# Where an expert block's bias enters PSUM: from a TensorE product to a ScalarE copy

## The chip, the cores and the metric

The kernel runs on one core of one Trainium2 chip. Its time is the device time of one execution in microseconds (us), given as the median of several runs. The profile is of one execution of its own, whose time stands beside its span below. PE is TensorE, ACT ScalarE, DVE VectorE, POOL GpSimd and SP SyncE.

## The reference

Two layers work on x (4 x 512 tokens, 512 channels): a gate and a Mamba2 mixer, a gate and a mixture of experts, a gate and grouped causal attention, a gate and a gated feed-forward network. The change touches the mixture of experts alone (8 experts, each token goes to its two best):

```python
logits = x @ gate_w.T + gate_b
top_vals, top_idx = jax.lax.top_k(logits, TOP_K)
routing = jax.nn.softmax(top_vals.astype(jnp.float32), axis=-1).astype(x.dtype)
for e in range(E):
    h = x @ w1[e].T + b1[e]
    x_glu = h[:, 0::2]
    x_lin = h[:, 1::2]
    y = x_glu * jax.nn.sigmoid(1.702 * x_glu) * (x_lin + 1.0)
    ye = y @ w2[e].T + b2[e]
    we = jnp.sum(routing * (top_idx == e), axis=-1)
    out = out + ye * we[:, None]
```

## The kernel before, in words

One core does the whole program; each engine has its own instruction list, written out by hand, and the lists meet at semaphores. The four stages follow one another. Within the expert stage the order is fixed by the Python code: nothing is planned by costs.

**Routing.** The gate logits, the top two and the prefix sums give each of the 4096 (token, expert) pairs a slot. The slots are sorted by expert and cut into 39 blocks (`NBLK`) of 128 slots, each of one expert. DVE writes a small integer table `tab` (one column for each block: its expert, the next expert, and a flag that says whether the next expert's weights must be split now). Engines read it with value loads into registers. During this the tokens are stored to DRAM as `u_tok` (SP, L621), behind the loads of the routing constants and of the bias table `bias_f` (L605 and L607).

**A block.** In block j PE (`block_pe`, L2372) does this in order: four transposes of block j's inner values `m_y` into the bank TP; the two up products of block j+1 (`up_glu`, `up_lin`) into banks UG and UL, three of each in turn; a wait for `by_lo` of block j; four transposes of the gathered tokens of block j+2 (`inputs_T`) into the same TP; the down product of block j into the bank DN. Each of the three products (`product`, L2344) is 12 matmuls of 128x128 weights on 512 columns in a split form (high times high, high times low, low times high) and, ahead of them, one bias product (L2345): a selector `sel_e` (which row is the block's expert) times the table `bias_r`. It opens the accumulation with start=True. So there are 39 x 3 = 117 bias products.

ACT (`block_act`, L1000) copies TP to `by_hi` (L1008), takes the tanh of UG into `m_t` (`up_tanh`, L977), copies TP to `bu_hi` (`u_hi_copy`, L981), and copies DN to `m_o` (L1036), which a DMA of its queue stores (L1043). DVE (`block_dve`, L1836) follows each with `by_lo` (L1842), `glu` into `m_t` (L1809), `inner` into `m_y` (L1815), the selector of block j+2 (L1803) and `bu_lo` (L1819), which PE needs for the next block. Where the flag is set, the next expert's weights are split too, in three pieces: the high parts on ACT (L990), the low parts on DVE (L1797), laced between the copies above. With this data these are blocks 0, 4, 18, 22, 23, 27 and 34.

ACT's list is a loop of six blocks (L1054), passed six times, and three blocks behind it; DVE's too (L1887). PE's loop holds three blocks (L2398). In the list of each ACT block stands an If with the weight pieces and an Else without them, and value loads of the table for the block behind (L997 and L998). At the loop's top the first of these loads stand ahead of the first block's `by_hi`: the blocks 0, 6, 12, 18, 24 and 30, and 36 behind the loop, are called heads here.

**Beside it** the recurrence of the next gate runs: scans on DVE (L449, L462), products and sums on POOL, a few copies and exps on ACT, DMAs of the queues of SP and ACT. POOL also gathers the tokens of each block with indirect DMAs (L752). SP loads the weights of each expert into `m_stage` (L616).

Of the kernel before, what the change touches and what calls it, by code (L numbers as in the profile page):

```python
# [19 lines left out]
P = 128  # L20
BATCH, T, C = 4, 512, 512
KC = C // P
# [25 lines left out]
for _name, _n in (("iota", P), ("before", P), ("rst", NT * E), ("rst2", NT * E), ("full", NT), ("blk", 2 * NT), ("place", 1), ("row", 1)):  # L48
    RC[_name] = _at
    _at += _n  # L50
# [41 lines left out]
def network(nc, xT, fT, condT, cols_d, rows_d, w_in_d, w_out_d, moe_d, gw_d, bias_d, rc_d, att_d, ffn_d, outT):  # L92
# [6 lines left out]
    with ctx:  # L99
# [75 lines left out]
        with ExitStack() as s:  # L175
            m_stage = sb("m_stage", [P, MOE_W], F32, s)
            mw = sb("mw", [P, 2, 2, MOE_W], F32R, s)
            ug = sb("ug", [P, 3, C], F32, s)
            bu_hi = sb("bu_hi", [P, KC, P], F32R, s)
            bu_lo = sb("bu_lo", [P, KC, P], F32R, s)  # L180
            m_t = sb("m_t", [P, I_MOE], F32, s)
            m_y = sb("m_y", [P, I_MOE], F32, s)
            by_hi = sb("by_hi", [P, KC, P], F32R, s)
            by_lo = sb("by_lo", [P, KC, P], F32R, s)
            m_o = sb("m_o", [P, 2, C], F32, s)
            sb("pad_b", [P, 256], F32, s)
            bias_r = sb("bias_r", [P, 2 * I_MOE + C], F32R, s)
            sel_e = sb("sel_e", [P, 3, P], F32R, s)
            row_e = sb("row_e", [P, 1], F32, s)
            exp_of = sb("exp_of", [P, NBLK + 1], F32, s)  # L190
            idx = sb("idx", [P, NBLK], I32, s)
            idx_now = sb("idx_now", [P, 3], I32, s)

            tab = sb("tab", [P, 3, NBLK + 1], I32, s)
        with ExitStack() as s:
# [4 lines left out]
            bias_f = sb("bias_f", [P, 2 * I_MOE + C], F32, s)  # L200
# [5 lines left out]
            etab = sb("etab", [P, 3, NBLK + 1], F32, s)  # L206
# [54 lines left out]
        masks_ready, setup_step, setup_mm, setup_act = sem("masks_ready"), sem("setup_step"), sem("setup_mm"), sem("setup_act")  # L261
# [26 lines left out]
        route_mm, route_vec, lg_exp = sem("route_mm"), sem("route_vec"), sem("lg_exp")  # L288
        LGP_DONE, U_DONE, PREFIX_DONE, IDX_DONE = 1, 2, 3, 4
        LG_SUB, MASK_READY, ONEHOT_READY, IDX_READY, TAB_READY = 1, 2, 3, 4, 5  # L290
        m_staged = [sem(f"m_staged{i}") for i in range(M_PIECES)]
        mw_hi_ready, w_split, sel_ready = sem("mw_hi_ready"), sem("w_split"), sem("sel_ready")
# [35 lines left out]
        AT_PREFIX, AT_POSITION, AT_ROWS = 38, 47, 51  # L328
# [16 lines left out]
        def keep_busy(n):  # L345

            for _ in range(n):
                nc.tensor.matmul(SPARE[:].rearrange("p (a l) -> p a l", a=TB), ident_b[:],
                                 causal_b[:].unsqueeze(1).to_broadcast([P, TB, P]), start=True, stop=True)
# [205 lines left out]
        def _(sp):  # L555
# [48 lines left out]
            sp.wait_ge(masks_ready, N_MASKS + 1)  # L604
            sp.dma_start(rc[:], rc_d).then_inc(loaded, 16)  # L605
            for h in range(2):
                sp.dma_start(bias_f[32 * h:32 * h + E, :], bias_d).then_inc(loaded, 16)  # L607

            def stage(e):

                for p in range(M_PIECES):
                    if not isinstance(e, int):
                        sp.wait_ge(w_split, M_PIECES * (e - 1) + p + 1)
                    src = moe_d[e] if isinstance(e, int) else moe_d[bass.ds(e, 1)].rearrange("o p w -> (o p) w")
                    o = slice(p * M_PIECE, (p + 1) * M_PIECE)
                    sp.dma_start(m_stage[:, o], src[:, o]).then_inc(m_staged[p], 16)  # L616


# [3 lines left out]
            with sp.Fori(1, E) as e:  # L622
                stage(e)

# [47 lines left out]
        def _(pool):  # L672
# [70 lines left out]
            done(nc.gpsimd.memset(bias_f[:], 0.0))  # L743

# [78 lines left out]
        def _(act):  # L823
# [11 lines left out]
            act.wait_ge(setup_mm, 1)  # L835
# [134 lines left out]
            A(ex[:], lg[:], ACT.Exp).then_inc(lg_exp, 1)  # L970
# [8 lines left out]
            def u_hi_copy(j):  # L979
                act.wait_ge(tu_done, j + 1)  # L980
                A(bu_hi[:].rearrange("p k t -> p (k t)"), TP[:], ACT.Copy).then_inc(bu_hi_ready, 1)  # L981

# [17 lines left out]
            def block_act(pair, h, q, nxt, last):  # L1000
# [9 lines left out]
                if last and q == 2:  # L1010
                    inner_hi()
                else:
                    flag, e = nxt
                    with act.If(flag != 0):
                        act.wait_ge(dn_done, FIRST + j)
                        split_hi(e, e % 2, (0,))
                        inner_hi()
                        split_hi(e, e % 2, (1,))
                        up_tanh(j + 1, (q + 1) % 3)
                        split_hi(e, e % 2, (2,))  # L1020
                        if not (last and q >= 1):
                            u_hi_copy(j + 2)
                    with act.Else():
                        inner_hi()
                        up_tanh(j + 1, (q + 1) % 3)
                        if not (last and q >= 1):
                            u_hi_copy(j + 2)
# [5 lines left out]
                nxt = next_expert(j + 1, last) if more else None  # L1033
                act.wait_ge(dn_done, FIRST + j + 1)
# [9 lines left out]
                return nxt  # L1044

            split_hi(0, 0)
# [5 lines left out]
            up_tanh(0, 0)  # L1052
            u_hi_copy(1)
            with act.Fori(0, NBLK // 6) as pair:  # L1054
                nxt = next_expert(pair * 6, False)
                for h in range(2):
                    for q in range(3):
                        nxt = block_act(pair, h, q, nxt, False)
            nxt = next_expert(NBLK - 3, True)
            for q in range(3):  # L1060
                nxt = block_act(NBLK // 6, 0, q, nxt, True)
# [205 lines left out]
        def _(dve):  # L1267
# [414 lines left out]
            for b in range(1, BATCH):  # L1682
                token_copies(dve, b)
                if b == 2:
                    dve.wait_ge(loaded, 64 + 48)
# [28 lines left out]
            dve.wait_ge(lg_exp, 1)  # L1714
# [55 lines left out]
            each(V.tensor_scalar(etab[:, 0, :], etab[:, 0, :], E - 1.0, None, ALU.min))  # L1770
            dve.wait_ge(route_mm, IDX_DONE)
# [6 lines left out]
            route.inc(V.tensor_copy(exp_of[:], etab[:, 0, :]))  # L1778
            route.inc(V.tensor_copy(row_e[:], rconst("row", 1)))
# [18 lines left out]

            def select(j, q):

                if not (isinstance(j, int) and j < 3):
                    dve.wait_ge(dn_done, FIRST + j - 2)
                V.tensor_scalar(sel_e[:, q, :], row_e[:].to_broadcast([P, P]), exp_of[:, bass.ds(j, 1)], None,  # L1803
                                ALU.is_equal).then_inc(sel_ready, 1)
# [72 lines left out]
            select(0, 0)  # L1877
            select(1, 1)
# [282 lines left out]
        def _(pe):  # L2161
# [5 lines left out]
            M(bank[0][:, 0:BATCH], ones[:], condT_s[:], start=True, stop=True).then_inc(setup_mm, 1)  # L2167
# [159 lines left out]
            pe.wait_ge(loaded, 64 + 48)  # L2327
# [5 lines left out]
            for at in (AT_PREFIX, AT_POSITION, AT_ROWS):  # L2333
                pe.wait_ge(dve_step, DVE_MAMBA * BATCH + at)
                keep_busy(8)
# [4 lines left out]
            keep_busy(8)  # L2340
# [3 lines left out]
            def product(out, x_hi, x_lo, slot, c0, q, bias):  # L2344
                M(out, sel_e[:, q, :], bias_r[:, bias:bias + C], start=True, stop=False)  # L2345
                for kc in range(KC):
# [3 lines left out]
                    M(out, x_hi[:, kc, :], hi, start=False, stop=False)  # L2350
                    M(out, x_hi[:, kc, :], lo, start=False, stop=False)  # L2351
                    mm = M(out, x_lo[:, kc, :], hi, start=False, stop=(kc == KC - 1))  # L2352
                return mm

            def up_glu(j, q, e, slot):
                pe.wait_ge(bu_split, j + 1)
                pe.wait_ge(sel_ready, j + 1)
                pe.wait_ge(w_split, M_PIECES * e + 1)
                product(UG[q][:], bu_hi, bu_lo, slot, 0, q, 0).then_inc(g_done, 1)

            def up_lin(j, q, e, slot):
                pe.wait_ge(w_split, M_PIECES * e + 2)
                product(UL[q][:], bu_hi, bu_lo, slot, M_PIECE, q, I_MOE).then_inc(l2_done, 1)
# [8 lines left out]
            def block_pe(it, q, last):  # L2372
# [15 lines left out]
                pe.wait_ge(out_copied, FIRST + j)  # L2388
                product(DN[:], by_hi, by_lo, e0 % 2, 2 * M_PIECE, q, 2 * I_MOE).then_inc(dn_done, 1)

            pe.wait_ge(route_vec, TAB_READY)
            keep_busy(12)
# [229 lines left out]
            with pe.Fori(0, FS // 2) as it:  # L2622
# [6 lines left out]
               w_in=(P, KC, IN_COLS), w_out=(P, XC, C), moe=(E, P, MOE_W), gw=(P, KC, E), bias=(E, 2 * I_MOE + C), rc=(P, N_RC),  # L2629
# [3 lines left out]
def routing_constants():  # L2633
# [5 lines left out]
                 blk=one * (np.arange(2 * NT) % NT), place=n[:, None], row=n[:, None] % 32)  # L2639
# [3 lines left out]
def lay_out(i):  # L2643
# [26 lines left out]
        bias=np.concatenate([b1[..., 0], b1[..., 1], i["L0_ffn_b2"]], axis=1), rc=routing_constants(), att=np.concatenate([wkv[0], wkv[1], wq, wd], axis=2), ffn=np.concatenate([up, down], axis=2))  # L2670
# [18 lines left out]
```

## Time and profile before

| | us |
|---|---|
| median of 3 runs | 2552.84 (2552.50 to 2559.88) |
| profiled execution | 2558.35 |
| its span in the trace | 2556.5 |
| expert stage, first up product to last down product | 836 to 1262 |
| PE busy, whole span | 2282.6 (89%) |
| ACT busy, whole span | 944.6 (37%) |
| DVE busy, whole span | 1874.8 (73%) |

The profiled execution's time is its span and 1.85 us around it; it is 5.5 us above the median. Matmuls overlap in the pipeline, so what one of them costs is the distance between two starts, not its duration. "<-issue" behind an idle time means that the engine waited for nothing that the profile shows: its sequencer was at register work, at a table load or at its next instruction. PEclk is the granted TensorE clock as a share of full speed (1.00 is 2.4 GHz, 0.50 is 1.2 GHz).

### The profile page before, as it was taken

How to read it: one execution, taken by the hardware profiler on the slowest of the kernel's cores; microseconds unless marked ns; L12 is line 12 of the kernel's file. 1: busy time of each engine (PE TensorE's matmuls, PEld its weight loads, DVE VectorE, ACT ScalarE, POOL GpSimd, SP SyncE). 2: the span in 40 equal slices, each digit the busy share in tenths (PEclk: the TensorE clock that was granted, in tenths of full speed). 3: DMA queues.
4: the chain of work that ended last, by engine and by line, in shares of the span. 5: the costliest groups of instructions: out<-in, count | busy, mean ns of one | idle time of the engine just before them, and what ended most of it. 6: DMA issues, size and time to landing. Idle time of an engine off the chain costs nothing.

```text
span 2556.5 us, 34018 instructions
## 1 busy us (share of the span) xinstructions
PE 2282.6 (89%) x10567; PEld 1688.2 (66%) x10568; DVE 1874.8 (73%) x2875; ACT 944.6 (37%) x1956; POOL 683.2 (27%) x545
## 2 busy tenths in 40 slices
PE   0789989989897899899878999999999988999998
PEld 0344444444455678778666888888888876788886
DVE  8989898889896765676545668768777785666665
ACT  3243342342432232342343444444434444322222
POOL 5434434343341443335331012122212210000000
PEclk9999999999998899999988999999999998999999
DMA  5000001010023432343241000010010101000001
GB/s 207 17 34 33 33 17 50 17 41 25 33 83 130 144 115 82 114 149 114 101 158 34 1 33 17 17 38 21 17 38 21 49 17 50 25 25 25 25 12 66
DMA packets 50502, 142.19 MB, mean 56 GB/s; under 512 B 4768, under 2 KB 4768, under 8 KB 46064
## 3 DMA queue, kind: packets, MB, share of 16 engines
q1 hardware_dynamic: 31872, 89.89, 10.0%
q10 hardware_dynamic: 12864, 32.81, 3.5%
q0 software_dynamic: 5680, 18.62, 2.4%
q14 instruction: 64, 0.52, 0.1%
q8 instruction: 22, 0.36, 0.1%
HBM read 106.95 MB, written 34.34 MB: 55 GB/s over the span
## 4 chain that ended last, share of the span: by engine, by line
PE 42%; issue 30%; POOL 10%; DVE 8%; POOLq 6%; ACT 3%; ACTq 0%; DMA 0%; DVEq 0%; another core or an unknown queue 0%
PE bank L341 9%; PE bank L343 9%; PE bank L342 9%; PE bank L2351 3%; PE bank L2352 3%; PE bank L2350 3%; PE bank L2304 3%; POOLq L494 2%; POOL g_v L495 2%; POOL g_v L502 2%; POOLq L520 1%; POOLq L517 1%; POOLq L506 1%; PE bank L2414 1%; POOL g_eu L501 1%
## 5 line engine op out<-in xcount | busy, mean ns | idle before, releaser
L2179 PE MATMUL bank<-um,w_in 128*128 128x512 f32 x576 | 263.5, 612 | 5.5 <-DVE lm L1515 5.3
L2179 PEld LDWEIGHTS bank<-um,w_in 128*128 128x128 f32 x576 | 110.0, 196 | 136.7 <-issue 128.5
L341 PE MATMUL bank<-u_hi,aw_hi 128*128 (+1 forms) x384 | 158.6, 413 | 12.9 <-DVE u_lo L1920 9.1
L1135 ACT ACTIVATE probs<-bank,nmx 128x128 f32<-128x128 f32 (+3 forms) x256 | 131.8, 528 | 91.6 <-DVE nmx L1943 91.6
L1142 ACT ACTIVATE pt_hi<-bank 128x512 fp32r<-128x512 f32 (+1 forms) x192 | 94.0, 526 | 165.0 <-PE bank L2304 163.8
L343 PE MATMUL bank<-u_hi,aw_lo 128*128 (+1 forms) x384 | 152.1, 396 | 0.0
L342 PE MATMUL bank<-u_lo,aw_hi 128*128 (+1 forms) x384 | 151.9, 396 | 0.0
L1958 DVE TENSOR_TENSOR pt_lo<-bank,pt_hi 128x512 fp32r<-128x512 f32 (+1 forms) x192 | 108.7, 593 | 42.5 <-ACT pt_hi L1142 41.1
L341 PE MATMUL bank<-u_hi,fw_hi 128*128 128x512 f32 x352 | 136.9, 389 | 0.0
L342 PE MATMUL bank<-u_lo,fw_hi 128*128 128x512 f32 x352 | 136.9, 389 | 0.0
L343 PE MATMUL bank<-u_hi,fw_lo 128*128 128x512 f32 x352 | 136.9, 389 | 0.0
L449 DVE TENSOR_TENSOR_SCAN g_s<-decay,g_s 128x512 f32<-128x512 f32 x96 | 128.1, 1375 | 10.5 <-POOL g_v L495 10.5
L501 POOL TENSOR_TENSOR g_eu<-g_eu,g_s 128x512 f32<-128x512 f32 x48 | 65.7, 1368 | 249.2 <-DVE g_s L462 249.2
L2304 PE MATMUL bank<-ident,probs 128*128 128x128 f32 x640 | 93.9, 278 | 42.0 <-DVE pt_lo L1958 19.6
L1940 DVE TENSOR_REDUCE rinv<-bank 128x1 f32<-128x128 f32 (+3 forms) x256 | 107.7, 484 | 31.4 <-PE bank L2456 31.2
L462 DVE TENSOR_TENSOR_SCAN g_s<-decay,g_s 128x512 f32<-128x512 f32 x96 | 112.3, 1211 | 20.3 <-issue 19.4
L2351 PE MATMUL bank<-mw,bu_hi 128*128 (+1 forms) x312 | 124.4, 399 | 0.0
L2352 PE MATMUL bank<-mw,bu_lo 128*128 (+1 forms) x312 | 124.2, 398 | 0.0
L2350 PE MATMUL bank<-mw,bu_hi 128*128 (+1 forms) x312 | 124.2, 398 | 0.0
L2127 DVE SCALAR_TENSOR_TENSOR XT<-bank,cols,XT 128x512 f32<-128x512 f32 x176 | 120.0, 744 | 3.4 <-PE bank L343 3.4
L2300 PE MATMUL bank<-xa,w_out 128*128 128x512 f32 x256 | 111.8, 592 | 0.0
L2304 PEld LDWEIGHTS bank<-ident,probs 128*128 128x128 f32 x640 | 73.4, 142 | 55.0 <-DVE probs L1952 23.0
(388 smaller groups left out, 6202.3 us busy)
## 6 DMA issues: line engine op xcount, KB each, us to landing
m_stage<-in_moe SPq DMA_DIRECT2D x21, 1024.0 KB, 5.3
y_slot<-m_o ACTq DMA_DIRECT2D x39, 256.0 KB, 2.7
g_v<-in_fT SPq DMA_DIRECT2D x18, 512.0 KB, 3.3
gates<-g_v SPq DMA_DIRECT2D x18, 512.0 KB, 2.8
f_stage<-in_ffn SPq DMA_DIRECT2D x11, 768.0 KB, 4.3
u_g<-gates SPq DMA_DIRECT2D x8, 1024.0 KB, 10.7
aw_in<-in_att SPq DMA_DIRECT2D x4, 1280.0 KB
w_in<-in_w_in ACTq DMA_DIRECT2D x1, 4640.0 KB, 16.8
```

Source lines behind the costliest of these rows:

```text
L341: nc.tensor.matmul(out, hi_w, hi_x, start=start, stop=False)
L342: nc.tensor.matmul(out, hi_w, lo_x, start=False, stop=False)
L343: return nc.tensor.matmul(out, lo_w, hi_x, start=False, stop=stop)
L449: nc.vector.tensor_tensor_scan(x, d, x, 0.0, ALU.mult, ALU.add).then_inc(g_vec, 1)
L462: nc.vector.tensor_tensor_scan(x[:, ::-1], d, x[:, ::-1], 0.0, ALU.mult, ALU.add).then_inc(g_vec, 1)
L1135: A(probs[:, h % 2, PR_AT[qb]:PR_AT[qb] + w], S_[bk][:, c0:c0 + w], ACT.Exp, bias=nmx[:, h % 2, qb:qb + 1], scale=SCALE, accum_out=rsum[:, ...
L2127: V.scalar_tensor_tensor(xm, FD[m][:], col("down_s", m), xm, ALU.mult, ALU.add).then_inc(fx_acc, 1)
L2179: mm = M(dst[:], w_in[:, k, c0:c0 + P], um[:, k, :], start=(k == 0), stop=(k == KC - 1))
L2304: return nc.tensor.transpose(out, src, ident[0:dim, 0:dim])
L2350: M(out, x_hi[:, kc, :], hi, start=False, stop=False)
L2351: M(out, x_hi[:, kc, :], lo, start=False, stop=False)
L2352: mm = M(out, x_lo[:, kc, :], hi, start=False, stop=(kc == KC - 1))
```

## The change

The bias products go. In their place ACT copies the bias of the block's expert into the bank before the 12 products, which now all accumulate (start=False): `fill_up` makes two copies, into UG and UL of block j+2, and `fill_dn` one, into DN of block j, with the scale 2 since `m_o` is copied with 0.5. PE waits for the counter `filled`. For the copies the bias must stand on all 128 partitions, so the table is now (8, 128, 1536) and loaded by expert, in steps of 512 KB (`up_bias`) and 256 KB (`dn_bias`, into a free part of `g_v`). ACT finds expert and buffer in a fourth row of `tab`, one load more for each block and three more at the loop's top. The selector, the table's split on DVE and a memset on POOL go; four small DVE operations on the table come. In the routing, seven filler matmuls open the seven banks once (`BITS_SET`), and SP's loop over the experts is written out.

```diff
@@ ACT
+            def fill_up(packed, q):
+
+                act.wait_ge(up_bias_in, packed % 8 * 16 + 16)
+                for t, half in ((UG, 0), (UL, 1)):
...
+                    A(t[q][:], src, ACT.Copy).then_inc(filled, 1)
+
+            def fill_dn(j, packed):
+
+                act.wait_ge(dn_bias_in, packed % 8 * 16 + 16)
+                act.wait_ge(out_copied, FIRST + j)
+                src = bias_dn[:, bass.ds(packed % 2, 1), :].rearrange("p o w -> p (o w)")
+                A(DN[:], src, ACT.Copy, scale=2.0).then_inc(filled, 1)
+
+            def packed_of(j, last):
+                at = tab[0:1, 3, j:j + 1] if last else tab[0:1, 3, bass.ds(j, 1)]
+                return act.value_load(at, min_val=0, max_val=8 * 2 + E - 1)
...
                         split_hi(e, e % 2, (0,))
                         inner_hi()
+                        fill_dn(j, packed[0])
                         split_hi(e, e % 2, (1,))
                         up_tanh(j + 1, (q + 1) % 3)
+                        if not (last and q >= 1):
+                            fill_up(packed[2], (q + 2) % 3)
                         split_hi(e, e % 2, (2,))
                         if not (last and q >= 1):
                             u_hi_copy(j + 2)
                     with act.Else():
                         inner_hi()
+                        fill_dn(j, packed[0])
                         up_tanh(j + 1, (q + 1) % 3)
                         if not (last and q >= 1):
+                            fill_up(packed[2], (q + 2) % 3)
                             u_hi_copy(j + 2)
...
             with act.Fori(0, NBLK // 6) as pair:
                 nxt = next_expert(pair * 6, False)
+                packed = [packed_of(pair * 6 + i, False) for i in range(3)]
@@ DVE
-                    each(V.tensor_scalar(bias_f[:, 2 * I_MOE:], bias_f[:, 2 * I_MOE:], 2.0, None, ALU.mult))
-                    each(V.tensor_copy(bias_r[:], bias_f[:]))
-                    route.inc(V.tensor_tensor(bias_r[32:32 + E, :], bias_f[32:32 + E, :], bias_r[32:32 + E, :].bitcast(F32), ALU.subtract))
...
-                    select(j + 2, (q + 2) % 3)
                     u_lo_split(j + 2)
@@ PE
-                M(out, sel_e[:, q, :], bias_r[:, bias:bias + C], start=True, stop=False)
...
-                pe.wait_ge(sel_ready, j + 1)
+                pe.wait_ge(filled, 2 if isinstance(j, int) and j == 0 else j * 3 + 1)
...
-                pe.wait_ge(out_copied, FIRST + j)
+                pe.wait_ge(filled, j * 3 + (3 if last and q == 2 else 5))
@@ SP, ahead of the token stores and in the loads of the weights
+            up_bias(0)
...
+                    if p == 0:
+                        up_bias(e)
+                        if e > 1:
+                            dn_bias(e - 1)
```

How ACT's list changes is shown at two places. The first is the top of its loop of six blocks, from the loop's entry to the If of the first block (TENSOR_LOAD is a value load, ISA a wait or register step). Before:

```order
L1054 UNCONDITIONAL_BRANCH
L1054 ISA
L997 TENSOR_LOAD tab
L997 ISA x2
L998 ISA
L998 TENSOR_LOAD tab
L998 ISA x2
L1014 COMPARE_AND_BRANCH
```

And with the change:

```order
L1099 UNCONDITIONAL_BRANCH
L1099 ISA
L1032 TENSOR_LOAD tab
L1032 ISA x2
L1033 ISA
L1033 TENSOR_LOAD tab
L1033 ISA x2
L1016 ISA
L1016 TENSOR_LOAD tab
L1016 ISA x3
L1016 TENSOR_LOAD tab
L1016 ISA x3
L1016 TENSOR_LOAD tab
L1016 ISA x2
L1050 COMPARE_AND_BRANCH
```

Three value loads more stand ahead of the first block. The second place is the Else of that block, the path of a block without weight pieces. Before:

```order
L1007 ISA
L1008 ACTIVATE by_hi<-bank 128x512
L974 REGISTER_ALU
L977 ACTIVATE m_t<-bank 128x512
L980 REGISTER_ALU
L981 ACTIVATE bu_hi<-bank 128x512
L1023 UNCONDITIONAL_BRANCH
```

And with the change:

```order
L1042 ISA
L1043 ACTIVATE by_hi<-bank 128x512
L1009 ISA
L1012 ISA
L1012 ACTIVATE bank<-g_v 128x512
L987 REGISTER_ALU
L990 ACTIVATE m_t<-bank 128x512
L998 ISA
L1005 ISA
L1005 ACTIVATE bank<-bias_u 128x512
L1005 ISA
L1005 ACTIVATE bank<-bias_u 128x512
L993 REGISTER_ALU
L994 ACTIVATE bu_hi<-bank 128x512
L1062 UNCONDITIONAL_BRANCH
```

The copy into DN stands between `by_hi` and the tanh, those into UG and UL between the tanh and `bu_hi`. In such rows, ACT's whole loop of six blocks has 203 before (L1054) and 321 with the change (L1099); for comparison, ACT's attention loop (L1222) has 281 in both, DVE's expert loop (L1887) 257 before and 233 with the change (L1922), DVE's Mamba loop (L1474) 367 in both.

## Rows read from the trace of the kernel before

**Rows 1.** Windows of 836 to 1262 and six blocks: busy per engine, PEclk, DMA share.
```profile
836.00:1262.00 426.00, 397.19 (x1824) 322.96 (x1825) 279.14 (x333) 141.94 (x199) 175.42 (x162) 0.96 0.33 113
...
918.41:977.25 58.84, 58.84 (x283) 48.62 (x282) 34.52 (x47) 16.53 (x29) 24.21 (x25) 1.00 0.22 71
```

**Rows 2.** PE waits in the expert stage, line and releaser: total us, times, longest.
```profile
PE bank L2304 <- DVE by_lo L1842: 12.5, 7, 5.4
```

**Rows 3.** Timeline of PE in a plain block: start, duration, line, out<-in.
```profile
1010.11 0.39 PE L2345 MATMUL bank<-bias_r,sel_e 128*128 128x512 f32 x1
1010.33 0.39 PE L2350 MATMUL bank<-mw,bu_hi 128*128 x1
```

**Rows 4.** Groups by line, whole span: ACT copies that write a PSUM bank.
```profile
L932 ACT ACTIVATE bank<-bank,dt 128x128 f32<-128x128 f32 x256 | 68.7, 355 | 75.1 <-PE bank L2248 74.8
```

**Rows 5.** Timeline of ACT in a plain block: tanh and bu_hi.
```profile
1020.11 0.60 ACT L977 ACTIVATE m_t<-bank 128x512 f32<-128x512 f32 x1 [1.47 <-PE bank L2352]
1023.50 0.60 ACT L981 ACTIVATE bu_hi<-bank 128x512 fp32r<-128x512 f32 x1 [2.79 <-PE bank L2304]
```

**Rows 6.** Timelines at the loop head of block 30: ACT, DVE, PE.
```profile
1178.54 0.60 ACT L1008 ACTIVATE by_hi<-bank 128x512 fp32r<-128x512 f32 x1 [2.71 <-issue]
...
1179.17 0.69 DVE L1842 TENSOR_TENSOR by_lo<-bank,by_hi 128x512 fp32r<-128x512 f32 x1 [2.22 <-ACT by_hi L1008]
...
1175.03 0.60 PE L2304 MATMUL bank<-ident,m_y 128*128 128x128 f32 x4
...
1181.40 0.60 PE L2304 MATMUL bank<-ident,ug 128*128 128x128 f32 x4
```

**Rows 7.** The two value loads at that head: duration, first and last start.
```profile
L997 ACTq TENSOR_LOAD <-tab x1: 555/555/555, 1176.8 to 1176.8; - x1
...
L998 ACTq SEQ_ASSERT  x1: 18/18/18, 1178.2 to 1178.2; - x1
```

**Rows 8.** The backward branch of ACT's expert loop, and the record behind it.
```profile
L1054 ACTq COMPARE_BRANCH  x1: 45/45/45, 1176.4 to 1176.4; - x1
L1054 ACTq FUSED_REGOPS  x1: 68/68/68, 1176.7 to 1176.7; - x1
```

**Rows 9.** The backward branch of ACT's attention loop, and ACT's next work.
```profile
L1222 ACTq COMPARE_BRANCH  x1: 45/45/45, 1700.9 to 1700.9; - x1
L1222 ACTq FUSED_REGOPS  x1: 50/50/50, 1704.5 to 1704.5; - x1
...
1704.58 0.60 ACT L1118 ACTIVATE vT<-bank 128x512 f32<-128x512 f32 x1 [4.18 <-issue]
```

**Rows 10.** The backward branch of DVE's Mamba loop.
```profile
L1474 DVEq COMPARE_BRANCH  x1: 56/56/56, 428.6 to 428.6; - x1
L1474 DVEq FUSED_REGOPS  x1: 85/85/85, 431.4 to 431.4; - x1
```

**Rows 11.** The backward branch of DVE's expert loop.
```profile
L1887 DVEq COMPARE_BRANCH  x1: 56/56/56, 1175.4 to 1175.4; - x1
L1887 DVEq FUSED_REGOPS  x1: 85/85/85, 1175.7 to 1175.7; - x1
```

**Rows 12.** PE's work after a wait, and windows behind two waits: PEclk.
```profile
1045.20 0.65 PE L2304 MATMUL bank<-ident,ug 128*128 128x128 f32 x4 [2.56 <-DVE by_lo L1842]
...
1046.40:1049.90 3.50, 3.50 (x10) 2.75 (x9) 3.40 (x6) 0.42 (x1) 1.92 (x2) 0.52 0.96 363
...
871.00:876.00 5.00, 4.36 (x13) 3.63 (x14) 4.89 (x7) 0.60 (x1) 4.15 (x4) 0.51 0.00 0
```

**Rows 13.** PE in block 4, which splits the next expert's weights.
```profile
907.99 0.66 PE L2304 MATMUL bank<-ident,m_y 128*128 128x128 f32 x4 [0.68 <-DVE bu_lo L1819]
```

**Rows 14.** All engines' waits, 770 to 836: the longest for a token store.
```profile
ACT ut L533 <- DMA u_tok<-ut: 14.5, 2, 13.8
```

**Rows 15.** Window of the first token stores: as rows 1 (DMA share, GB/s last).
```profile
777.00:792.00 15.00, 14.90 (x58) 10.60 (x59) 5.63 (x6) 0.62 (x2) 5.19 (x4) 0.55 0.96 340
```

**Rows 16.** DVE in the routing, before the indices.
```profile
827.96 0.20 DVE L1772 COPY idx_f<-bank 128x39 f32<-128x39 f32 x1 [0.36 <-PE bank L2338]
```

More of the change, by code:

```diff
@@ L47 @@
 _at = 0
-for _name, _n in (("iota", P), ("before", P), ("rst", NT * E), ("rst2", NT * E), ("full", NT), ("blk", 2 * NT), ("place", 1), ("row", 1)):
+for _name, _n in (("iota", P), ("before", P), ("rst", NT * E), ("rst2", NT * E), ("full", NT), ("blk", 2 * NT), ("place", 1)):
     RC[_name] = _at
@@ L621, in _ @@
                 sp.dma_start(u_dram[a * P:(a + 1) * P, :], ut[:, a % 4, :]).then_inc(ut_stored[a % 4], 16)
-            with sp.Fori(1, E) as e:
+            sp.wait_ge(g_out[0], FIRST_DMA + 16 * ((G_MOE + 1) // 2))
+            dn_bias(0)
+            for e in range(1, E):
                 stage(e)
+            sp.wait_ge(w_split, M_PIECES * (E - 1) + 1)
+            dn_bias(E - 1)
             sp.wait_ge(dn_done, FIRST + NBLK)
@@ L2166, in _ @@
             pe.wait_ge(loaded, 64)
-            M(bank[0][:, 0:BATCH], ones[:], condT_s[:], start=True, stop=True).then_inc(setup_mm, 1)
+            M(bank[0][:, 0:BATCH], ones[:], condT_s[:], start=True, stop=True).then_inc(route_mm, 1)
             pe.wait_ge(masks_ready, N_MASKS)
@@ L2332, in _ @@
             M(LGP[:, 256:384], ones[:], gt2, start=True, stop=True).then_inc(route_mm, 1)
-            for at in (AT_PREFIX, AT_POSITION, AT_ROWS):
+            for i in range(2):
+                pe.wait_ge(ut_copied[i], NT // 2)
+            pe.wait_ge(dve_step, DVE_MAMBA * BATCH + AT_PREFIX)
+            for into in (*UG, *UL, DN):
+                mm = keep_busy(1, into)
+            mm.then_inc(route_mm, 1)
+            for at in (AT_POSITION, AT_ROWS):
                 pe.wait_ge(dve_step, DVE_MAMBA * BATCH + at)
-                keep_busy(8)
+                keep_busy(8, UL[2])
             pe.wait_ge(route_vec, ONEHOT_READY)
@@ L2339, in _, with product @@
             mm.then_inc(route_mm, 1)
[L2340 to L2345 removed]
+            keep_busy(8, UL[2])
+            def product(out, x_hi, x_lo, slot, c0):
                 for kc in range(KC):
@@ L2387, in block_pe @@
                 pe.wait_ge(w_split, M_PIECES * (e0 + 1))
-                pe.wait_ge(out_copied, FIRST + j)
-                product(DN[:], by_hi, by_lo, e0 % 2, 2 * M_PIECE, q, 2 * I_MOE).then_inc(dn_done, 1)
+                pe.wait_ge(filled, j * 3 + (3 if last and q == 2 else 5))
+                product(DN[:], by_hi, by_lo, e0 % 2, 2 * M_PIECE).then_inc(dn_done, 1)
             pe.wait_ge(route_vec, TAB_READY)
-            keep_busy(12)
+            keep_busy(12, UL[2])
             inputs_T(0, 0, 0)
@@ L2638, in routing_constants @@
                  rst2=one * (np.arange(NT * E) % NT > 0), full=one * np.where(np.arange(NT) == 0, -1, P * np.arange(NT)),
-                 blk=one * (np.arange(2 * NT) % NT), place=n[:, None], row=n[:, None] % 32)
+                 blk=one * (np.arange(2 * NT) % NT), place=n[:, None])
     return np.concatenate([parts[k] for k in RC], axis=1).astype(np.float32)
```

107 lines of the change are left out of this document (58 added, 49 removed).

## The prediction

> **What bounds the kernel now.** I read the windows first. In the expert stage PE is busy 397.19 of 426.00 us, ACT only 141.94, and six blocks without weight pieces run without any gap: 58.84 us with 58.84 busy, so 9.81 us for a block, all of it PE [rows 1]. There a product that is taken from PE comes off the time. The 28.8 us that PE is idle are waits, and the list of waits shows for what: most of all for `by_lo`, 12.5 us in seven waits, the longest 5.4 [rows 2]. `by_lo` is DVE's, straight behind ACT's `by_hi`, so wherever ACT is late, PE stops. The change moves work from PE to ACT; the timelines of ACT must say whether ACT has room at each place where it gets more. What matters then is not ACT's mean load (a third of the stage) but the few microseconds between two deadlines.
>
> **What comes off.** In a gap-free stretch a bias product starts at 1010.11 and the next product at 1010.33 [rows 3]: 0.22 to 0.23 us; I take 0.227, the mean over its twelve neighbours at 0.22 and 0.23. A block has three: 0.68 us, 9.81 becomes 9.13. I count the blocks 2 to 38; the first two wait for a chain of scans (one of the waits for `by_lo`, the 5.4) and gain nothing. 37 x 0.68 = **25.2 us** off.
>
> **The copies in a plain block.** The trace has no 128x512 copy from SBUF to PSUM. The nearest: the same shape from PSUM to SBUF takes 0.60 us [rows 5]; 128x128 written into a bank takes 0.355 [rows 4], which at four times the columns would be at most 1.42. I take 0.60, the row of the same shape. ACT is idle for 1.47 us before the tanh, where the copy into DN goes, and for 2.79 before `bu_hi`, where the two others go [rows 5]. 0.6 fits into the first and 1.2 into the second with some tenths of register steps; at 1.42 the first still just fits and the second is 0.1 late, which PE doesn't see. Cost 0. Each copy also waits for its bias to have landed. Queued behind such a wait are the tanh or `bu_hi`, and behind those DVE's `m_y` and `bu_lo`, for which PE waits at the next block; but the bias is loaded an expert ahead, so only the close pair of experts below can show it. The one value load more in each block stands in ACT's idle time before `m_o`: also 0.
>
> **The heads.** Here ACT has no room. At the head of block 30 PE starts its transposes of `m_y` at 1175.03, ACT copies `by_hi` only at 1178.54, with 2.71 us idle "<-issue", `by_lo` runs from 1179.17 to 1179.86, and PE needs it at 1181.40 [rows 6]: 1.5 us of slack. The idle time is the branch back and the two value loads. Both grow:
> - Loads: the two take 1.4 us, from 1176.8 to 1178.2, and the first has 0.555 us in its read alone [rows 7]. That is 0.7 on the mean; I take 0.6 for each further one, since the read is the floor and the first has the loop's set-up with it. Three more: 1.8 us (2.1 at most).
> - The branch: from the compare to the first record at the top are 0.3 us now [rows 8]. Of ACT's attention loop, 281 rows long, the same pair is 3.6 us apart, and ACT's next work shows 4.18 us "<-issue" [rows 9]. DVE's Mamba loop (367 rows) pays 2.8 [rows 10], DVE's expert loop (257 rows) 0.3 [rows 11]. So a short loop comes back at once and a long one pays for its instructions again. The change takes ACT's expert loop from 203 rows to 321: from the side of the short ones to that of the long ones. Bounds 0 and 3.25 us more; I take 3.25, the row of the same engine.
>
> Rows 9 show ACT paying at the branch of a loop of 281 rows. The Trainium skill (Runtime: NRT & Kernel Launch, Instruction fetch mechanics) says that each engine but PE has an instruction memory of 512 instructions in two pages of 256, and that a taken branch whose target is outside that window waits for a DMA. By the number 512, the changed loop would still fit and the branch would stay at 0.3 us; but so would the attention loop, which by rows 9 it doesn't. I go by the row, and keep the page's reading as a rival.
>
> Then `by_hi` comes at 3.51 + 1.8 + 3.25 = 8.56 us behind the start of the transposes, `by_lo` ends at 8.56 + 0.63 + 0.69 = 9.88. PE, with two bias products fewer, wants it at 6.37 - 0.45 = 5.92. A wait of 3.96 us. Behind such waits the clock falls: after 2.56 us the next 3.50 us ran at a granted 0.52, after the 5.4 the 5.00 us from 871 at 0.51 [rows 12], the lower level of 1.2 GHz. 3.50 us at 0.52 cost 1.7, 5.00 at 0.51 cost 2.45; I take 1.7. So a head costs 5.66, and there are four plain ones entered by the branch (6, 12, 24, 30): **22.6**.
> Block 18 is a head with weight pieces, where PE waits for ACT and DVE already: 1.8 + 3.25, its 0.68 not gained, and one fill of 0.6 in the chain: **6.3**.
> Block 36 is entered without a branch back: `by_lo` ends at 9.88 - 3.25 = 6.63 instead of 5.92, **0.7**.
>
> **The other blocks with weight pieces** (4, 22, 23, 27, 34) end on DVE's chain of pieces, as in block 4, where PE waits 0.68 us for `bu_lo` [rows 13]. A shorter PE only waits longer: 5 x 0.68 = **3.4**. That the fills come later into that chain and the selector leaves it I set against each other.
>
> **Ahead of the stage.** The token stores hold ACT for up to 13.8 us [rows 14], in a window in which the DMA engines move 340 GB/s at a share of 0.96 [rows 15]. 512 KB of bias go in ahead of them: 0.52 / 0.34 = 1.5 us (0 if the queues have room, 3.0 if the stores behind them go at half that rate for as long). In the routing four operations like the 0.20 us one go in ahead of it, where 0.36 us were idle [rows 16]: 0.4. Together **1.9**. The table's split on DVE there and the memset on POOL are hidden by these stores: 0. The other bias loads, 768 KB for each expert beside 3 MB of weights, go behind the first weight piece: 0, up to 2.2 us at one close pair of experts (0.75 MB at 340 GB/s).
>
> **Sum.** 22.6 + 6.3 + 0.7 + 3.4 + 1.9 - 25.2 = +9.7 us. Against the profiled execution: 2558.35 + 9.7 = 2568.0. That one is 5.5 above the median, so against the median: **2562.5 us**.
>
> **Rivals.**
> *The loop still comes back at once* (chance 0.22). For it: the branch costs nothing for 257 rows, and of the 321 one path of each If is skipped. Against it: rows 9, with 281. Then only the loads are left: a wait of 0.71 at four heads (2.8), 3.05 at block 18, and 0.7 + 3.4 + 1.9: 11.9 - 25.2 = -13.3, **2539.5**, faster. It decides by the branch alone: below about 1.5 us the change is faster by more than a measurement can tell. The page named above stands on this side.
> *The branch costs DVE's 2.5 us more, and the clock stays up* (0.22). For it: rows 10, in which the longer of the two loops pays the shorter time. Against it: they are another engine's, and 2.56 us of wait already brought a dip [rows 12]. 4 x 3.23 + 5.6 + 0.7 + 3.4 + 1.9 = 24.5: -0.7, **2552.1**, no change.
> *Heavier* (0.08): dips of 2.45 (3.0 more) and the 2.2 us of bias loads: **2567.7**.
> *The copies don't fit* (0.02): PE would wait for `filled` in each plain block. Only above 1.4 us a copy.
>
> **The numbers.** The forecast (branch and dips as above) has 0.46. Its own range is 2557 to 2568, from the bounds of the start and the dips. The range over all reaches from the first rival to the heavier case with 3.0 at the start, rounded: 2538 to 2570. A measurement of this kernel tells 0.3%, 7.7 us, from no change: faster is below 2545.2, slower above 2560.5. Faster 0.23 (the first rival); slower 0.46: most of the forecast's case and the heavier one; same 0.31, the second rival and the forecast's low end.
>
> **What would show it.** In the changed trace: the gap behind the compare of ACT's expert loop, 3.5 or 0.3 us, and with it packets of the instruction queue in each pass; `by_hi` at heads some 8.5 us behind PE's transposes; waits of PE for `by_lo` of some 4 us at four heads, and PEclk at 0.5 behind them; six plain blocks at 9.13 us each; copies into a bank of 0.6 us; nowhere a wait of PE for ACT's fills. I am wrong if the plain blocks stay at 9.8 (the copies are on the path), or if the branch's gap stays at 0.3.

## The result and the profile after

The changed kernel takes 2580.98 us (median of 4, 2579.11 to 2582.97) against 2554.45 us of the kernel before beside it: the ratio is 1.0101, 95% interval 1.0086 to 1.0116. A second measurement with more runs gave 1.0089 (1.0076 to 1.0103). It is slower by 23 to 26 us, about 1.0%, clear of its interval and on the side that was forecast, but 18 us beyond the forecast of 2562.5 and outside the range up to 2570. A ratio that is given below can differ by up to 0.0013 from the quotient of the two medians beside it; so differences of 3 us between two kernels are not certain. One single run stands far apart, 7896.11 us of c_ahead (experiment 1): its ratio leaves it out, its median of 2532.5 us counts it.

The windows of the changed kernel: the expert stage, and 45 us of plain blocks in it (busy time per engine, PEclk, DMA share, GB/s):

```profile
836.00:1285.00 449.00, 380.88 (x1710) 306.06 (x1709) 265.56 (x296) 198.94 (x315) 166.68 (x161) 0.93 0.34 118
...
933.00:978.00 45.00, 45.00 (x216) 36.95 (x215) 24.95 (x31) 20.88 (x39) 17.27 (x19) 1.00 0.24 76
```

They answer [rows 1]. PE has 16 us less to do in the stage, and the stage is 23 us longer. The plain blocks are still gap-free, and shorter: `m_o` of blocks 7 and 11 stand at 941.74 and 978.48, 9.19 us for a block, where it was 9.81. So the part that the change aims at works. PE's list of waits says where the loss is:

```profile
PE bank L2339 <- DVE by_lo L1879: 48.1, 11, 9.3
```

48.1 us in eleven waits, where [rows 2] has 12.5 in seven. Here is ACT at the head of block 12, which comes by the branch back, by its timeline:

```profile
978.48 0.60 ACT L1078 ACTIVATE m_o<-bank 128x512 f32<-128x512 f32 x1
979.56 0.34 ACTq L1085 DMA_DIRECT2D y_slot<-m_o  x1
988.46 0.60 ACT L1043 ACTIVATE by_hi<-bank 128x512 fp32r<-128x512 f32 x1 [9.38 <-issue]
988.95 0.60 ACT L1012 ACTIVATE bank<-g_v 128x512 f32 x1
989.47 0.59 ACT L990 ACTIVATE m_t<-bank 128x512 f32<-128x512 f32 x1
989.95 1.12 ACT L1005 ACTIVATE bank<-bias_u 128x512 f32 x2
991.07 0.60 ACT L994 ACTIVATE bu_hi<-bank 128x512 fp32r<-128x512 f32 x1
```

The copies into the banks take 0.60 us each, as assumed, and cost nothing. But ACT waits 9.38 us for nothing that a semaphore explains, where [rows 6] has 2.71. Its sequencer shows two stops, one behind the branch and one behind the first value load (lines 1099 and 1032; duration, first and last start):

```profile
L1099 ACTq COMPARE_BRANCH  x1: 54/54/54, 980.0 to 980.0; - x1
L1099 ACTq FUSED_REGOPS  x1: 68/68/68, 983.2 to 983.2; - x1
...
L1032 ACTq TENSOR_LOAD <-tab x1: 298/298/298, 983.3 to 983.3; - x1
L1032 ACTq FUSED_REGOPS  x1: 164/164/164, 985.5 to 985.5; - x1
```

From the compare to the first record at the top are 3.2 us ([rows 8]: 0.3). Then the value load is read in 0.3, and the next step comes 2.2 us after its start. In the same stretch the DMA view of the changed kernel, 980.0 to 986.5, has

```profile
q14 instruction: 4, 0.03, 1.7%
```

where the same stretch of the kernel before has no packet of the instruction queue. They are of 8 KB each, and each of the five passes by the branch brings four up to `by_hi`; the whole span has 97 packets of this queue instead of 64. PE's transposes then wait 5.56 us for `by_lo` (at the head in [rows 6] they waited for nothing), and the clock falls behind it (timeline of PE, and a window):

```profile
989.92 1.11 PE L2339 MATMUL bank<-ident,ug 128*128 128x128 f32 x4 [5.56 <-DVE by_lo L1879]
...
989.92:993.50 3.58, 3.58 (x11) 3.03 (x12) 3.18 (x5) 1.74 (x4) 1.20 (x2) 0.55 0.00 0
```

A table of all blocks comes from the starts of `m_o` (L1036 before, L1078 after). Each number is the distance between two of them, in us; "head" is the distance that holds the head's wait.

| | before | after | difference |
|---|---|---|---|
| head 6 | 9.90 | 16.97 | +7.07 |
| head 12 | 9.90 | 16.47 | +6.57 |
| head 18 (with weight pieces) | 14.26 | 21.30 | +7.04 |
| head 24 | 9.83 | 20.12 | +10.29 |
| head 30 | 9.89 | 17.64 | +7.75 |
| the 32 others, up to the `m_o` of block 37 | 342.06 | 327.45 | -14.61 |

Five blocks of 37 lose 38.7 us, the other 32 win 14.6, 24.1 remain. (Blocks 0 and 38 and the other stages are not in the table; the two spans are 22.3 us apart.)

### The profile page after: what moved, and what is told of

Same layout as the page of the kernel before. It is cut to its first block, busy times and chain, and to the rows that moved or that the text cites. A ratio compares the mean times of both kernels' runs of the same rounds, so it can differ in the third digit from the quotient of the medians.

```text
span 2578.8 us, 34195 instructions
## 1 busy us (share of the span) xinstructions
PE 2272.5 (88%) x10449; PEld 1672.1 (65%) x10450; DVE 1859.4 (72%) x2835; ACT 1002.0 (39%) x2073; POOL 676.6 (26%) x544
## 4 chain that ended last, share of the span: by engine, by line
PE 37%; issue 31%; POOL 11%; DVE 8%; POOLq 6%; ACT 3%; DMA 1%; ACTq 1%; DVEq 0%; SPq 0%; another core or an unknown queue 0%
PE bank L340 9%; PE bank L341 9%; PE bank L342 9%; PE bank L2339 3%; POOLq L495 2%; POOL g_v L503 2%; POOL g_v L496 2%; PE bank L2390 2%; PE bank L2391 2%; PE bank L2392 2%; POOLq L521 1%; PE bank L2454 1%; POOLq L518 1%; POOLq L507 1%; POOL g_s L517 1%
## 5 line engine op out<-in xcount | busy, mean ns | idle before, releaser
L1288 ACT ACTIVATE f_t<-bank,f_sc 128x512 f32<-128x512 f32 x44 | 30.2, 687 | 209.5 <-PE bank L342 208.8
## 6 DMA issues: line engine op xcount, KB each, us to landing
u_g<-gates SPq DMA_DIRECT2D x8, 1024.0 KB, 10.1
```

## The experiments

Theory A: ACT's loop has outgrown what its instruction memory keeps, and each pass fetches it again. Rivals: B, the copies and the three more value loads themselves make ACT late; C, the added loads of the biases do. Counted in single instructions, which the rows of the lists above partly bundle ("ISA x2"), ACT's loop has 248 before and 388 with the change.

**1. No loop on ACT, loads ahead.** (label c_ahead)

```diff
-            with act.Fori(0, NBLK // 6) as pair:
-                nxt = next_expert(pair * 6, False)
-                packed = [packed_of(pair * 6 + i, False) for i in range(3)]
+            for pair in range(NBLK // 6):
+                if pair == 0:
+                    nxt = next_expert(0, True)
+                    packed = [packed_of(i, True) for i in range(3)]
...
-                more = (q < 1) if last else (h, q) != (1, 2)
-                nxt = next_expert(j + 1, last) if more else None
-                ahead = [packed_of(j + 3, last)] if (q < 0 if last else (h, q) != (1, 2)) else []
+                nxt = next_expert(j + 1, True) if j + 1 <= NBLK - 2 else None
+                ahead = [packed_of(j + 3, True)] if j + 3 < NBLK else []
...
-            nxt = next_expert(NBLK - 3, True)
-            packed = [packed_of(NBLK - 3 + i, True) for i in range(3)]
```

> The change with ACT's list of the expert stage written out, block by block, without its loop, so that no branch goes back and the value loads of each block stand in the idle time of the one before. Theory A (ACT's loop has outgrown its instruction memory and each pass fetches it again, 3.2 us at the branch and 1.9 us behind the first value load): five head blocks fall from 16.5 to 21.3 us to the 9.2 us of a plain one (13.5 for the one with weight pieces), 42 us in all: 2539 us. Theory B (the copies and the value loads themselves make ACT late at the heads): most of the loss stays, 2565 to 2580 us. Theory C (the added bias traffic delays the heads): it stays too, 2575 to 2580 us.

Measured: 2532.5 us, beside 2551.51 of before: 0.9927 (0.9907 to 0.9947). A second measurement with more runs, below, has 0.9918. The heads are now like other blocks; ACT at the one of block 12, by its timeline:

```profile
971.16 0.59 ACT L1077 ACTIVATE m_o<-bank 128x512 f32<-128x512 f32 x1
971.78 0.34 ACTq L1084 DMA_DIRECT2D y_slot<-m_o  x1
972.58 0.60 ACT L1043 ACTIVATE by_hi<-bank 128x512 fp32r<-128x512 f32 x1 [0.82 <-ACT m_o L1077]
```

`by_hi` comes 1.42 us behind `m_o` instead of 9.98, and block 12 takes 9.12 us, head 18 with its weight pieces 11.21. The copies, their waits and the bias loads are all still in. So C, and the copies of B, fall as causes of most of the loss. The edit takes away two things, the branch back and the value loads at the heads; which of them made the loss, this run can't tell.

**2. The loop, with the loads at the heads, written out.** (label c_unroll) Only the line with `act.Fori` is changed to `for pair in range(NBLK // 6)`.

> The change with ACT's list of the expert stage written out without its loop, but with the five value loads still ahead of the first block of every six, as in the change. It parts the fetch from the loads. Theory A (the fetch of ACT's instructions is the loss): by_hi of a head comes 5.3 us behind PE's transposes in place of 9.8, 0.7 us after PE wants it, at six heads: 2532.5 us of the version that loads ahead, and 4 to 6 us: 2537 us. Theory B (the value loads are the larger part): 2555 us or more.

Measured: 2536.05 us, 0.9941 (0.9924 to 0.9958). `by_hi` of heads 6, 12 and 30 comes 4.1 to 4.4 us behind `m_o`; the block that holds the head takes 9.01, 9.26 and 9.21 us. PE waited 1.42 us at head 6 and not at all at 12 and 30; head 18 takes 14.61, against 11.21 with the loads ahead. Against the two measurements of c_ahead the ratio is 0.0014 and 0.0023 higher: the value loads at the heads cost some 4 to 6 us in all, with intervals that overlap. That is B's share.

**3. The control: the kernel before, written out.** (label b_unroll) The same one line in the kernel before.

> The kernel before with ACT's loop of the expert stage written out in the same way: the control. The loop of before is not fetched again and its heads have 1.5 us of slack, so theory A expects nothing from it: 2551.5 us within 2 us. If writing ACT's list out were worth something by itself (a rival for what the written-out change gained), it would be faster by 5 us or more.

Measured: 2549.74 us beside 2551.55, 0.9983 (0.9971 to 0.9994). Writing the list out is worth 2 us by itself by the medians, 4 by the ratio, not 20. In the trace most of it is at head 18, 11.66 us in place of 14.26.

**4. The loop of before, made long.** (label b_pad)

```diff
-                return (act.value_load(entry(2, j), min_val=0, max_val=1),
+                return (act.value_load(entry(2, j), min_val=0, max_val=3),
...
+                if not last:
+                    with act.If(nxt[0] > 1):
+                        for _ in range(7):
+                            act.value_load(tab[0:1, 0, bass.ds(j, 1)], min_val=0, max_val=E - 1)
                 more = (q < 1) if last else (h, q) != (1, 2)
```

> The kernel before, with a body in each block of ACT's loop that is never entered (seven value loads behind a flag that is never above 1): the loop has 392 instructions in place of 248, the change's has 388, and what is executed grows by one branch a block. Theory A: the loop is fetched again at each pass, ACT is 5 us late at five heads, of which 1.5 us are slack, and the clock falls behind the wait: +20 to +28 us, 2575 to 2582 us, with instruction packets in each pass. Theories B and C: within 2 us of the kernel before, 2554 us.

Measured: 2557.45 us, 1.0023 (1.0014 to 1.0033): +6 us, where A said 20 to 28. The branch of this kernel:

```profile
L1058 ACTq COMPARE_BRANCH  x1: 45/45/45, 978.7 to 978.7; - x1
L1058 ACTq FUSED_REGOPS  x1: 68/68/68, 981.5 to 981.5; - x1
```

2.8 us instead of 0.3, with instructions that are never executed: the length alone brings the fetch, so A's mechanism is shown. But the price is small. The blocks of heads 6, 12 and 30 take 11.66, 11.51 and 11.36 us, +1.5 to 1.8. ACT comes 3.0 us later, 1.5 us are slack, and PE waits the other 1.3 to 1.6 us. Head 18 costs 2.4 us (16.63), and head 24, where the fetch meets a weight load, 5.2 (15.00). Behind the value load there is no second stop: the step after it comes 0.3 us on. But there is one further on, between the compare of the If and the first record of its Else:

```profile
L1014 ACTq COMPARE_BRANCH  x1: 45/45/45, 982.7 to 982.7; - x1
L1007 ACTq FUSED_REGOPS  x1: 46/46/46, 983.7 to 983.7; - x1
```

It is 0.9 us here, 1.1 and 0.8 at the heads 6 and 30 and 2.3 at head 24; the kernel before has 0.2. So the fetch alone makes ACT 3 us late. At head 12 of the change `by_hi` is 6.65 us later than before (9.98 us behind `m_o` in place of 3.33): 2.9 are the branch, 1.6 the stop behind the first value load, 1.8 the three further loads, and 0.3 stand ahead of the branch. Only the first 1.5 us of such a sum are slack.

**5. The change with the loop's top 12 instructions further on.** (label c_shift)

```diff
+            for i in range(4):
+                packed_of(i, True)
             with act.Fori(0, NBLK // 6) as pair:
```

> The change with four value loads more, once, ahead of ACT's loop: its top stands 12 instructions further on. In the change ACT stops twice at each pass, 3.2 us behind the branch and 1.9 us behind the first value load, four instructions below the top. Theory A2 (the second stop is the crossing into the next block of instructions that is fetched): with the top moved over that edge it goes, by_hi of four heads comes 2 us sooner, and with the shorter waits 10 us are won: 2568 to 2572 us. Theory A1 (the second stop is the value load's own, behind a branch): nothing moves, 2579 us.

Measured: 2557.84 us beside 2551.55, 1.0024 (1.0013 to 1.0035), the most surprising run: four loads more, and by the ratios to before 17 to 20 us less than the change. The records at the top (lines 1101 and 1032):

```profile
L1101 ACTq COMPARE_BRANCH  x1: 54/54/54, 982.2 to 982.2; - x1
L1101 ACTq FUSED_REGOPS  x1: 68/68/68, 985.0 to 985.0; - x1
...
L1032 ACTq TENSOR_LOAD <-tab x1: 300/300/300, 985.1 to 985.1; - x1
L1032 ACTq FUSED_REGOPS  x1: 164/164/164, 985.4 to 985.4; - x1
```

The second stop is gone, and the first is 2.8 us instead of 3.2. A2 holds: the change's loop top lay just ahead of an edge in what is fetched at a time, and ACT waited once for each side of it. The run before fits the same edge. Count ACT's instructions from the start of its list, from 0: the top is number 322 in the change, and ACT stops behind number 323 (the expectation says four below the top; it is the second). In b_pad the top is 311, the compare of the If 319 and the first instruction of the Else 338: ACT crosses the same place by that jump, and stops there. Here the top is 334, behind it. And up to `by_hi` of head 12 there are four instruction packets in the change, three in b_pad and two here.

The effect is twice what was expected. `by_hi` comes 2.4 to 3.7 us sooner at all five heads, 13.9 in all, where 2 us at four were expected; the heads together take 18.9 us less, so at some the clock adds to it. `by_hi` of head 12 comes 2.64 us sooner, and PE's wait falls from 5.56 to 2.90 us. Windows of this kernel behind the waits of heads 6, 12 and 18 (4.88, 2.90 and 6.85 us):

```profile
929.86:933.40 3.54, 3.54 (x11) 2.96 (x12) 3.14 (x5) 1.74 (x4) 1.20 (x2) 0.50 0.00 0
989.80:993.30 3.50, 3.50 (x18) 2.96 (x19) 3.17 (x5) 1.67 (x4) 1.20 (x2) 1.00 0.00 1
1052.14:1056.00 3.86, 3.86 (x11) 3.22 (x12) 3.76 (x4) 3.26 (x4) 1.82 (x2) 0.50 0.89 318
```

Behind 2.90 us the clock stayed at 2.4 GHz, behind the longer waits it ran at 1.2. So 2.64 us of ACT's lateness were worth 4.10 us at head 12 (16.47 to 12.37), and 5.33 at head 30 (17.64 to 12.31).

**6. The change with a shorter loop.** (label c_dedup)

```diff
                     with act.If(flag != 0):
                         act.wait_ge(dn_done, FIRST + j)
                         split_hi(e, e % 2, (0,))
-                        inner_hi()
-                        fill_dn(j, packed[0])
+                    inner_hi()
+                    fill_dn(j, packed[0])
+                    with act.If(flag != 0):
                         split_hi(e, e % 2, (1,))
-                        up_tanh(j + 1, (q + 1) % 3)
...
-                    with act.Else():
...
```

> The change with ACT's If and Else of a block made into three short Ifs around copies that stand once: the loop has 314 instructions in place of 388, and executes the same work with two branches more a block. Theory A: if 314 fit, the branch costs 0.3 us and the time is 2545 to 2550 us (loads at the heads remain); if they do not, as ACT's attention loop with 295 does not, fewer pages come again and the time is 2560 to 2580 us. Theories B and C: no change from the changed kernel, 2581 us, or 2 us more for the branches.

Measured: 2570.41 us, 1.0075 (1.0058 to 1.0092). 314 instructions don't fit either: the branch takes 2.8 us at four heads and 7.1 at head 24, and the step behind the first value load comes 1.9 to 2.0 us behind its start (2.8 at head 24), as in the change, whose top stands at the same place. Heads 12, 24 and 30 take 16.00, 21.97 and 16.32 us. By the ratios it is 4 to 7 us better than the change, and far from the 2545 us that a loop without fetches would have given. Here making the loop somewhat shorter was of little use while its top lay badly.

**7. No bias at all.** (label b_nobias)

```diff
-                M(out, sel_e[:, q, :], bias_r[:, bias:bias + C], start=True, stop=False)
...
-                    M(out, x_hi[:, kc, :], hi, start=False, stop=False)
+                    M(out, x_hi[:, kc, :], hi, start=(kc == 0), stop=False)
```

> The kernel before without the 117 bias products and without anything in their place (the biases are left out of the sums; the first of the 12 products opens the bank). It measures what the products cost: by the sum of the prediction 25.2 us less 3.4 us of blocks that wait for DVE anyway: 2532 to 2534 us under all three theories. If PE were not what bounds the plain blocks, less.

Measured: 2540.75 us, 0.9958 (0.9941 to 0.9975), 10.8 us where 18 to 20 were expected: the expectation was wrong. Some plain blocks take 10.0 to 10.1 us, with a wait of 0.5 for `by_lo`. In the timeline of DVE in one of them:

```profile
938.23 2.34 DVE L462 TENSOR_TENSOR_SCAN g_s<-decay,g_s 128x512 f32<-128x512 f32 x2 [1.82 <-issue]
940.48 0.66 DVE L1842 TENSOR_TENSOR by_lo<-bank,by_hi 128x512 fp32r<-128x512 f32 x1
941.07 0.67 DVE L1809 SCALAR_TENSOR_TENSOR m_t<-m_t,bank 128x512 f32<-128x512 f32 x1
941.84 0.69 DVE L1815 SCALAR_TENSOR_TENSOR m_y<-bank,m_t 128x512 f32<-128x512 f32 x1
942.45 0.80 DVE L1803 TENSOR_SCALAR sel_e<-row_e,exp_of 128x128 fp32r<-128x128 f32 x1
943.17 0.68 DVE L1819 TENSOR_TENSOR bu_lo<-bank,bu_hi 128x512 fp32r<-128x512 f32 x1
```

Behind the scans DVE is without a gap up to `bu_lo`, for which PE waits at the next block, and 0.7 us of that is the selector.

**8. No bias and no selector.** (label b_nobias_nosel) Besides, the calls of `select` and PE's wait for `sel_ready` are left out.

> The kernel before without the bias products and without DVE's 39 selectors either (the biases are left out of the sums). With the selectors still there, the same kernel gained 10.8 us, and its plain blocks beside two scans took 10.0 to 10.1 us with a wait for by_lo. Theory D (with PE at 9.13 us a block DVE bounds those blocks, and the selector's 0.3 to 0.8 us lies on that path): they fall to 9.3 us and the time to 2530 to 2534 us. Rival: the wait has another cause (POOL or gathers), and the time stays at 2540 us.

Measured: 2533.34 us, 0.9916 (0.9899 to 0.9933). The blocks of 10.0 to 10.1 us take 9.2 to 9.4. Theory D holds: 7 us by the medians, 11 by the ratios, of what moving the bias off PE brings come from DVE's selector, which goes with it. A kernel with no bias work at all is at 0.9916, and the written-out change, which computes everything, at 0.9918 to 0.9927. But the written-out list has 2 to 4 us of its own (experiment 3), so the two can't be compared to the microsecond: ACT's 117 copies, with the bias loads, cost a few microseconds at most.

**9. The bias loads thinned.** (label c_thin)

```diff
-                sp.dma_start(bias_u[:, e % 3, :], bias_d[e][:, 0:2 * I_MOE]).then_inc(up_bias_in, 16)
+                sp.dma_start(bias_u[:, e % 3, 0:(8 if e > 2 else 2 * I_MOE)], bias_d[e][:, 0:(8 if e > 2 else 2 * I_MOE)]).then_inc(up_bias_in, 16)
```

(and the down part in the same way from expert 2 on).

> The change with the bias loads of the experts 3 to 7 cut to 8 columns of each part (from expert 2 on for the part of the down product), so that their waits stay and nearly all of their 768 KB go; those experts' sums then use the biases of earlier experts. Theory C (the added bias traffic makes part of the loss): the head at block 24, where the instruction fetch takes 5.7 us beside a weight load, comes down from 20.1 us towards the 17 us of the others, and the time falls by 3 to 6 us. Theory A alone (only the fetch of the longer loop): less than 2 us, near 2580 us, with the head at 24 slow from the weight loads that before has too.

Measured: 2578.17 us, 1.0076 (1.0061 to 1.0091). The change beside it (experiment 10) has 2582.92: 4.75 us less by the medians, 3 by the ratios, whose intervals overlap. In time it is what C said, but not at the place it said. Head 24 takes 19.53 instead of 20.20 us. The branch still takes 5.8 us there, and only the second stop is shorter: the step behind the value load comes 2.2 instead of 3.2 us on. So the bias loads add about 1 us to the slow fetch at this head, and the 5.8 us stay without them; that the weight loads of a megabyte each make these was not tried. Of the rest the traces show where it is: blocks 5 and 19, each behind weight pieces, take 10.68 and 10.70 us, where the change beside it has 12.91 and 13.08. But the first profile of the change has 11.80 and 10.61 there, so it is not shown that the bias loads make this difference.

**10 and 11. The change and the written-out version again, side by side.** (labels after_again, c_ahead_again)

> The change itself, once more, beside the kernel before and the written-out version on one chip, for the comparison of the three: 2580 us, 1.010 of before.

> The change with ACT's list written out and the value loads ahead, once more in five rounds: 2532 us, 0.992 to 0.993 of before.

Measured: 2582.92 us, 1.0089 (1.0076 to 1.0103), and 2537.36 us, 0.9918 (0.9904 to 0.9931), beside 2558.42 us. The edit that takes ACT's loop and the value loads at its heads away turns 24.5 us of loss into 21 us of gain.

## Why the prediction was right in kind and too low

**The plain blocks: right.** 9.19 us where 9.13 were said. The copies take 0.60 us, fit into ACT's idle time, and PE nowhere waits for them. The 32 other blocks of the table together won 14.6 us, where the sum had 17.0 for them (26 at 0.68, less 0.7 for block 36). 22 of them are plain and neither have weight pieces nor follow such a block; they won 12.9, mostly 0.5 to 0.7 each; why some won less than 0.68 was not traced.

**The heads: right as a mechanism, 13 us too small.** The sum had 4.98 us more for each plain head (5.66 less 0.68) and 5.6 for head 18, 25.6 in all. They measured 38.7. By terms:
- The branch: 3.25 us more were said, from the attention loop [rows 9]; 2.9 to 3.1 were measured at four heads. At head 24 it was 5.4 more (5.7 us), in a stretch in which a weight load keeps the DMA engines busy (share 0.91, 338 GB/s). The prediction had taken one price for all. That is 2 us of the missing 13.
- **The step that failed is the one that made the fetch a single stop at the branch.** The trace of the change shows a second one behind the first value load: 1.6 to 1.9 us above the 0.3 that the step takes undisturbed, 2.9 at head 24. It was not in the sum, and not in the range: the bounds "0 and 3.25" were taken from loops whose rows show no second stop. In [rows 9] ACT's next work begins 0.1 us behind the first record at the top. The five second stops make 9.7 us of lateness, against the missing 13; c_shift shows that they go when the top is moved. With them the head waits are 5.6 to 9.3 us, where 3.96 were said.
- Value loads: 0.6 us each were said and measured (985.8 to 988.2 for the last four). In c_unroll, where they stand alone, they cost little (PE waits 1.42 us at head 6, 0.4 at head 24 and nothing at 12 and 30), as the first rival had it with its waits of 0.71 us.
- The clock: 1.7 us a head were said. 3.58 us at 0.55 behind head 12 are 1.6, and behind the other four heads of the change PEclk is 0.50 or 0.51 too. The term was right for the waits of 5.6 us and more that came.

**What is kept of a loop: right.** Loops of 388, 392 and 314 instructions on ACT were fetched again at each pass, that of 248 was not, as [rows 8] and [rows 9] had it. The Trainium skill (Runtime: NRT & Kernel Launch, Instruction fetch mechanics) gives engines like this one room for 512 instructions. By that number alone all of these loops would fit, and the runs contradict that use of it. The same section warns that a taken branch out of the two pages held waits for a DMA; that is what they show, with 2.8 us and instruction packets in b_pad.

**Ahead of the stage: wrong sign, small.** +1.9 us were said. ACT's longest wait for the stores stayed at 13.85 us (13.82 before), so the 512 KB cost nothing that shows there. From the last gate store of SP ahead of them (780.98 and 779.46) to the first up product (836.62 and 834.58) it is 55.64 us before and 55.12 after. Which of the things that went or came there (the memset, the table's split, the four small operations) made the 0.5 us was not tried.

**The rivals.** The one without a fetch said 13.3 us less than before, with the loads still at the heads. That is c_unroll, which has 15.5 us less than the kernel before beside it, 2 to 4 of them from writing the list out: the rival's sum was good, and its condition, a branch that costs nothing, did not come true in the change. The second rival fell with the branch's 3.2 us and with the clock. "Heavier" (2567.7) had the right sign with the wrong items. A rival with two stops was missing.

## What to carry to other kernels

When work is added to an engine, count its instructions too, not only its busy time: a loop that is a little too long (on ACT here 295 instructions and more; 248 were kept) is fetched again at each pass, and the price falls at its top, where the first instruction of a pass may be what another engine waits for. Look at the backward branch and at the first few records behind it, and at the slack of the loop's first deadline. If the count is near the limit, write the loop out, or at least try its top at another place: here four idle value loads ahead of it were worth 17 to 20 us, and the loop written out, with its loads moved ahead, 44 to 46.

## What was not expected of the hardware

- The same loop of 388 instructions stops ACT twice a pass at one place in the program, for 3.2 to 3.4 us and for 1.6 to 1.9 more, and once, for 2.8 us, 12 instructions further on (head 24 left out).
- Behind a wait of 2.90 us the granted clock stayed at 1.00, behind 4.88 us in the same kernel it was 0.50, and in the kernel before it was 0.52 behind 2.56 us [rows 12]. So the length of the wait alone does not say it; what else decides was not tried.
- The same branch took 3.2 us at a DMA share of 0.24 and 5.7 us at head 24, beside a weight load, at 0.91. In all four other kernels whose loop is fetched again head 24 is the slowest too, but by very different amounts: 3.4 us in b_pad (at 0.91), 5.2 in c_shift, 5.8 in c_thin and 7.1 in c_dedup. That the fetch waits for the bulk load is the likely reason, not a tested one.
